# Cross-attention operands of a two-layer decoder: projected unpadded and placed by DMA, against projected in place with padding

## The reference, cut to what matters

```python
# x (2, 512, 256), ctx (2, 1024, 192); 16 heads in both attentions
x = layernorm(x + L0_attn(x))      # causal, 3-wide heads, geo bias
x = layernorm(x + L0_xattn(x, ctx))
def L0_xattn(query, kv):           # D = 16, scale = D ** -0.5
    q = (query @ Wq + bq).reshape(B, 512, 16, 16)
    k = (kv @ Wk + bk).reshape(B, 1024, 16, 16)
    v = (kv @ Wv + bv).reshape(B, 1024, 16, 16)
    attn = softmax(clip(q k^T * scale, -10000, 10000))
    return (attn v) @ Wo + bo
```

## Time and profile before

| | us |
|---|---|
| median of 3 runs (1264.87 to 1274.17) | 1266.02 |
| the profiled execution | 1272.5 |
| its span, first to last instruction | 1270.6 |
| PE busy | 1150.3 (91%) |
| DVE busy | 719.7 (57%) |
| ACT busy | 565.0 (44%) |
| POOL busy | 105.4 (8%) |
| cross-attention's last maximum (L1454) begins | 513.4 |

### The profile page before, as it was taken

The page is one execution under the profiler, slowest core; times in us unless marked ns, Lnnn a source line. Parts: engine busy times, 40 slices in busy tenths (PEclk is TensorE's granted clock), DMA queues, the critical chain, the costliest instruction groups (busy, mean ns, idle before and its releaser), DMA issues.

```text
span 1270.6 us, 19991 instructions
## 1 busy us (share of the span) xinstructions
PE 1150.3 (91%) x7418; PEld 720.2 (57%) x7418; DVE 719.7 (57%) x1054; ACT 565.0 (44%) x1084; POOL 105.4 (8%) x147
## 2 busy tenths in 40 slices
PE   4999999898988988869988999999999999998797
PEld 2453443442222322247866777877787887786465
DVE  4344445667888789661426466465646666673213
ACT  1344344154545555751214566456635564562210
POOL 0112232112100000010001000010001000100100
PEclk7799899898979999979999999999999999999799
DMA  7012212320000000000023233123634964400000
GB/s 205 14 51 100 89 37 100 115 76 1 1 1 1 1 1 1 1 18 1 1 67 112 62 91 74 34 52 83 150 85 100 214 144 101 101 18 1 1 17 17
DMA packets 56962, 74.20 MB, mean 58 GB/s; under 512 B 12443, under 2 KB 33446, under 8 KB 56870
## 3 DMA queue, kind: packets, MB, share of 16 engines
q1 hardware_dynamic: 53110, 69.26, 21.4%
q10 hardware_dynamic: 3760, 3.67, 0.9%
HBM read 36.20 MB, written 15.73 MB: 41 GB/s over the span
## 4 chain that ended last, share of the span: by engine, by line
PE 79%; DVE 9%; issue 5%; ACT 4%; DMA 1%; POOL 1%; SPq 1%; ACTq 0%; POOLq 0%; DVEq 0%
PE p_unit L1665 20%; PE p_ring L1665 12%; PE p_out L1789 9%; PE p_ring L1685 8%; PE p_ring L1766 8%; PE p_ring L1732 7%; PE p_out L1755 6%; DVE halves L1454 2%; PE p_unit L1857 2%; PE p_ring L1710 1%; ACT prob_b L1238 1%; DVE prob_a L1468 1%; DVE x L1560 1%; PE p_ring L1724 1%; PE p_ring L1703 1%
## 5 line engine op out<-in xcount | busy, mean ns | idle before, releaser
L1454 DVE TENSOR_REDUCE halves<-p_ring 128x2 f32<-128x1024 f32 x128 | 156.2, 1220 | 65.8 <-PE p_ring L1710 65.6
L1252 ACT ACTIVATE prob_a<-p_ring 128x1024 f32<-128x1024 f32 x128 | 130.6, 1022 | 101.6 <-PE p_ring L1732 101.4
L1434 DVE TENSOR_REDUCE nmax<-p_ring 128x2 f32<-128x1024 f32 (+1 forms) x128 | 156.0, 1219 | 33.7 <-PE p_ring L1685 33.6
L1270 ACT ACTIVATE probT_b<-p_ring 128x512 f32<-128x512 f32 x144 | 84.5, 598 | 202.2 <-PE p_ring L1766 200.7
L1238 ACT ACTIVATE prob_b<-p_ring,nmax 128x512 f32<-128x512 f32 (+1 forms) x192 | 158.6, 837 | 18.3 <-DVE nmax L1434 18.0
L1685 PE MATMUL p_ring<-stacks 128*128 128x512 f32 x512 | 151.4, 418 | 8.9 <-ACT prob_b L1238 5.3
L1487 DVE COPY probT_b<-p_ring 128x512 f32<-128x512 f32 x112 | 77.1, 688 | 133.5 <-PE p_ring L1766 133.0
L1766 PE MATMUL p_ring<-ident,prob_b 128*128 128x128 f32 x1024 | 134.5, 274 | 0.3 <-ACT probT_b L1270 0.3
L1766 PEld LDWEIGHTS p_ring<-ident,prob_b 128*128 128x128 f32 x1024 | 116.2, 141 | 23.5 <-issue 14.8
L1732 PE MATMUL p_ring<-x_q,x_kq 32*128 32x512 f32 x512 | 124.4, 658 | 2.9 <-DVE halves L1454 2.9
L1454 DVE TENSOR_REDUCE wide_max<-p_ring 128x2 f32<-128x256 f32 (+3 forms) x64 | 52.6, 823 | 90.3 <-PE p_ring L1703 90.3
(11 more groups left out here) (226 smaller groups left out, 1614.1 us busy)
## 6 DMA issues: line engine op xcount, KB each, us to landing
stacks<-x_kd SPq DMA_DIRECT2D x64, 256.0 KB, 5.9
stacks<-splitH_b SPq DMA_DIRECT2D x80, 128.0 KB, 2.3
stacks<-splitL_b SPq DMA_DIRECT2D x80, 128.0 KB, 2.4
x_kd<-early SPq DMA_DIRECT2D x19, 256.0 KB, 2.0
x_v<-x_vd SPq DMA_DIRECT2D x8, 512.0 KB, 4.1
x_kd<-xT SPq DMA_DIRECT2D x13, 256.0 KB, 2.0
x_vd<-early SPq DMA_DIRECT2D x11, 256.0 KB, 2.0
a_st<-a_image SPq DMA_DIRECT2D x64, 32.0 KB, 1.8
```

Of the source, the lines that this page charges most:

```text
L1252: nc.scalar.activation(prob_place(key), slot_of("S2", key), ACT.Exp, accum_out=x0_sums[:, m:m + 1]).then_inc(done["E2"], 1)
L1270: keep_turned(act, key, lambda o, i: nc.scalar.activation(o, i, ACT.Copy)).then_inc(done["VA"], 1)
L1434: nc.vector.tensor_reduce(nmax[:, n % 4, 0:heads], src, AX.X, ALU.max, negate=True).then_inc(done["M"], 1)
L1454: nc.vector.tensor_reduce(to, src, AX.X, ALU.max, negate=True).then_inc(done["M1"], 1)
```

## The change

Keys and queries are projected with the weights as they come, unpadded: a key unit "kd" yields 128 rows (8 heads) by 512 keys, a query unit "qd" 128 rows by 512 queries. That makes 4 key units and 2 query units per batch. The keys go through an early place to DRAM (x0_kd, step XO), the queries stay in x0_qd; the scale is applied when ACT empties them. A new step KL on SP places a group: for each head one DMA for 16 rows of 1024 keys and one for 16 rows of 512 queries. GpSimd clears x0_kq once, to 1 where keys go and 0 where queries go, and casts a whole group in one instruction of 1536 columns (KF). The four key units of batch 0 take the turns of the first four before; those of batch 1 stand at the head of x1_context. A query unit of batch 1 waits until the KL that read the same half of batch 0 is three turns old. The padded weights, their staging tiles, their clearing and most of XW go. The matmuls of A0's scores read 32 rows, not 17. X0's scores read 32 rows before and after; the rows of keys that were 0 are now 1, against 0 in the queries.

```diff
--- before.py
+++ after.py
@@ -168,7 +168,7 @@
-        return age("KF", "q", L, b, g) >= 2 and all(age("KF", "k", L, b, g, h) >= 2 for h in range(2))
+        return age("KF", b, g) >= 2
...
-            if u[0] in ("k", "q") and u[1] == "X0":
-                sched.add("KF", *u)
-            if u[:2] == ("v", "X1"):
+            if u[:2] == ("v", "X1") or u[0] == "kd":
                 sched.add("XO", *u)
...
-    def x0_keys(b, g):
+    def x0_keys(b):
+        return [unit("kd", b, m, s) for m in range(2) for s in range(2)]
+
+    def x0_queries(b):
+        return [unit("qd", b, m, after=[turned_x("A0", b)] + ([later(("KL", (0, 2 * m + 1)), 3)] if b else [])) for m in range(2)]
+
+    def x0_operands(b, g):
         n = 4 * b + g - HELD
-        return [unit("k", "X0", b, g, h, after=used(8 + n) if n >= 0 else []) for h in range(2)]
-
-    def x0_queries(b, g):
-        n = 4 * b + g - HELD
-        return [unit("q", "X0", b, g, after=[turned_x("A0", b)] + (used(8 + n) if n >= 0 else []))]
+        return [step("KL", b, g, after=[UA("qd", b, g // 2), later(("XO", ("kd", b, g // 2, 1)), 1)]
+                     + (used(8 + n) if n >= 0 else [])),
+                step("KF", b, g, after=[later(("KL", (b, g)), 2)])]
...
+        order = [u[1][1:] for u in x0_keys(1)] + order
...
-        [unit("cT", sg, c) for sg in range(2) for c in range(2)] + x0_keys(0, 0) + x0_keys(0, 1)
-        + [unit("cT", sg, c) for sg in range(2, 4) for c in range(2)] + x0_keys(0, 2)
-        + x0_keys(0, 3) + [u for g in range(4) for u in x0_keys(1, g)],
-        [q for b in range(B) for g in range(4) for q in x0_queries(b, g)],
+        [unit("cT", sg, c) for sg in range(2) for c in range(2)] + x0_keys(0)
+        + [unit("cT", sg, c) for sg in range(2, 4) for c in range(2)],
+        [q for b in range(B) for q in x0_queries(b)],
+        [s for b in range(B) for g in range(4) for s in x0_operands(b, g)],
...
-                slot = sum(early_uses) % EARLY
+                slot = sum(early_uses) % (3 if u[:2] == ("kd", 0) else EARLY)
...
-        x0_wq = put("x0_wq", [128, 2, 512])
-        x0_wk0 = put("x0_wk0", [128, 512])
-        x0_wk1 = put("x0_wk1", [128, 512])
+        x0_wq = put("x0_wq", [128, 2, C])
+        x0_wk0 = put("x0_wk0", [128, C])
+        x0_wk1 = put("x0_wk1", [128, C])
+        x0_qd = put("x0_qd", [128, 2, T])
...
+        x0_kd = nc.dram_tensor("x0_kd", (B, C, NKV), F32).ap()
...
-        X0_LOADS = 12
+        X0_LOADS = 9
...
-            sp.dma_start(wq_in[:, :, :], rows("L0_xattn_Wq")).then_inc(x0_loaded, 16)
-            sp.dma_start(wk_in[:, 0, :], d["L0_xattn_Wk"][0:128, :]).then_inc(x0_loaded, 16)
-            sp.dma_start(wk_in[0:CC - 128, 1, :], d["L0_xattn_Wk"][128:CC, :]).then_inc(x0_loaded, 16)
-            sp.dma_start(wk_in[64:65, 1, :], d["L0_xattn_bk"].rearrange("(o n) -> o n", o=1)).then_inc(x0_loaded, 16)
+            sp.dma_start(x0_wq[:, :, :], rows("L0_xattn_Wq")).then_inc(x0_loaded, 16)
             sp.wait_ge(pads_cleared, 1)
-            sp.dma_start(x0_wv0[:, 0:C], d["L0_xattn_Wv"][0:128, :]).then_inc(x0_loaded, 16)
-            sp.dma_start(x0_wv1[0:CC - 128, 0:C], d["L0_xattn_Wv"][128:CC, :]).then_inc(x0_loaded, 16)
-            sp.dma_start(x0_wv1[64:65, 0:C], d["L0_xattn_bv"].rearrange("(o n) -> o n", o=1)).then_inc(x0_loaded, 16)
-            bq = d["L0_xattn_bq"].rearrange("(g a p) -> a p g", a=4, p=16)
-            for a in range(4):
-                sp.dma_start(x0_bq[32 * a:32 * a + 16, :], bq[a], allow_slow_non_contiguous=True).then_inc(x0_loaded, 16)
+            for w0, w1, n in ((x0_wk0, x0_wk1, "k"), (x0_wv0, x0_wv1, "v")):
+                sp.dma_start(w0[:, 0:C], d["L0_xattn_W" + n][0:128, :]).then_inc(x0_loaded, 16)
+                sp.dma_start(w1[0:CC - 128, 0:C], d["L0_xattn_W" + n][128:CC, :]).then_inc(x0_loaded, 16)
+                sp.dma_start(w1[64:65, 0:C], d["L0_xattn_b" + n].rearrange("(o n) -> o n", o=1)).then_inc(x0_loaded, 16)
+            sp.dma_start(x0_bq[:, :], d["L0_xattn_bq"].rearrange("(m p) -> p m", p=128),
+                         allow_slow_non_contiguous=True).then_inc(x0_loaded, 16)
...
                 if kind == "XO":
+                    if u[0] == "kd":
+                        _, b, m, s = u
+                        wait(sp, "UA", *u)
+                        sp.dma_start(x0_kd[b, 128 * m:128 * m + 128, 512 * s:512 * s + 512], early_place(u, 0))\
+                          .then_inc(early_out[early_places[(u, 0)][0]], 16)
+                    elif u[0] == "v":
...
-                        for part, ready in ((1, "EH"), (0, "EL")):
-                            wait(sp, ready, *u)
+                        wait(sp, "EL", *u)
+                        for part in (1, 0):
                             sp.dma_start(x1_kd[b, p, 1 - part, :, 512 * s:512 * s + 512], early_place(u, part))\
                               .then_inc(early_out[early_places[(u, part)][0]], 16)
+                if kind == "KL":
+                    b, g = key
+                    G, place = 8 + 4 * b + g, (4 * b + g) % HELD
+                    sp.wait_ge(x0_cleared, 1)
+                    for s in range(2):
+                        slot, before = early_places[(("kd", b, g // 2, s), 0)]
+                        sp.wait_ge(early_out[slot], 16 * (before + 1))
+                    wait(sp, "UA", "qd", b, g // 2)
+                    if 4 * b + g >= HELD:
+                        wait(sp, "S2", *prob_items(PAIRS[G - HELD])[-1])
+                    for a in range(4):
+                        sp.dma_start(x0_kq[32 * a:32 * a + 16, place, 0:2, :],
+                                     x0_kd[b, 64 * g + 16 * a:64 * g + 16 * a + 16, :].rearrange("r (s n) -> r s n", s=2))\
+                          .then_inc(x0_held[place], 16)
+                        at = 64 * (g % 2) + 16 * a
+                        sp.dma_start(x0_kq[32 * a:32 * a + 16, place, 2, :], x0_qd[at:at + 16, g // 2, :])\
+                          .then_inc(x0_held[place], 16)
...
             blank(a0_v).then_inc(values_cleared, 1)
-            pool.wait_ge(x0_scaled, 1)
+            nc.gpsimd.memset(x0_kq[:, :, 0:2, :], 1.0)
+            nc.gpsimd.memset(x0_kq[:, :, 2, :], 0.0).then_inc(x0_cleared, 1)
             blank(x0_v).then_inc(values_cleared, 1)
...
                 if kind == "KF":
-                    u = key
-                    _, L, b, g = u[:4]
-                    place, part = (4 * b + g) % HELD, u[4] if u[0] == "k" else 2
-                    wait(pool, "UA", *u)
-                    if 4 * b + g >= HELD:
-                        wait(pool, "S1", *max_items(PAIRS[8 + 4 * b + g - HELD])[-1])
-                    nc.gpsimd.tensor_copy(x0_kqF[:, place, part, :], x0_kq[:, place, part, :]).then_inc(done["KF"], 1)
+                    b, g = key
+                    n = 4 * b + g
+                    pool.wait_ge(x0_held[n % HELD], 16 * 8 * (n // HELD + 1))
+                    if n >= HELD:
+                        wait(pool, "S1", *max_items(PAIRS[8 + n - HELD])[-1])
+                    nc.gpsimd.tensor_copy(x0_kqF[:, n % HELD], x0_kq[:, n % HELD]).then_inc(done["KF"], 1)
...
-                    elif u[0] in ("q", "k") and u[1] == "X0":
-                        _, L, b, g = u[:4]
-                        place, part = (4 * b + g) % HELD, u[4] if u[0] == "k" else 2
-                        if 4 * b + g >= HELD:
-                            wait(act, "S2", *prob_items(PAIRS[8 + 4 * b + g - HELD])[-1])
-                        if u[0] == "q":
-                            ins = nc.scalar.activation(x0_kq[:, place, part, :], p_unit[:, :], ACT.Identity,
-                                                       bias=x0_bq[:, g:g + 1])
-                        else:
-                            ins = nc.scalar.activation(x0_kq[:, place, part, :], p_unit[:, :], ACT.Copy)
-                    elif u[:2] in (("k", "X1"), ("v", "X1")):
+                    elif u[0] == "qd":
+                        _, b, m = u
+                        act.wait_ge(x0_scaled, 1)
+                        if b:
+                            for g in (2 * m, 2 * m + 1):
+                                act.wait_ge(x0_held[g % HELD], 16 * 8 * (g // HELD + 1))
+                        ins = nc.scalar.activation(x0_qd[:, m, :], p_unit[:, :], ACT.Identity, bias=x0_bq[:, m:m + 1],
+                                                   scale=LAYERS["X0"]["D"] ** -0.5)
+                    elif u[:2] in (("k", "X1"), ("v", "X1")) or u[0] == "kd":
                         early_free(act, u, 0)
                         ins = nc.scalar.activation(early_place(u, 0), p_unit[:, :], ACT.Copy)
...
-            for t in (x0_wv0, x0_wv1):
+            for t in (x0_wk1, x0_wv0):
                 nc.vector.memset(t[:, :], 0.0)
-            nc.vector.memset(x0_bq[:, :], 0.0).then_inc(pads_cleared, 1)
+            nc.vector.memset(x0_wv1[:, :], 0.0).then_inc(pads_cleared, 1)
...
-            nc.vector.memset(x0_wq[:, :, :], 0.0)
```

(37 more changed lines are left out.)

22 lines of the change are left out of this document (4 added, 18 removed).

## The result

| | us | ratio to the kernel before |
|---|---|---|
| before, median beside the changed kernel | 1266.9 | |
| changed, median of 4 runs (1235.13 to 1245.31) | 1239.1 | 0.977 [0.975, 0.980] |
| changed, second comparison (a1_after) | 1243.2 | 0.980 [0.977, 0.983] |
| changed, third comparison (a2_after) | 1240.2 | 0.978 [0.975, 0.981] |

The change gains 24 to 28 us. I forecast 14.7, with a range that reached to a gain of 24 (1242 us).

What follows compares the result with a forecast made beforehand. PE was taken to bound self-attention, DVE cross-attention from about 300 us. Terms -22.1 + 1.4 + 3.4 - 1.8 + 4.4 gave -14.7 us, a predicted median of 1251.3 us; 8-in-10 range 1242 to 1263.

Steps and rivals of the forecast that it cites:

- -22.1 + 1.4 + 4.4: DVE-bound cross-attention: products gone -22.1 us, one query product of batch 1 coming back at turn 107 +1.4, casts +4.4.
- What bounds the kernel: PE bounds self-attention (60 to 200 us), DVE cross-attention from about 300; windows: DVE busy 29.79 of 31, 29.62 of 35 us.
- Products gone from five blocks: Cross-attention, turns 104 to 168: all 15 key and query products leave, saving 22.1 us (bounds 20.9 and 23.9).
- Early products: PE-bound part: seven products added, five removed, net 3.4 us more (bounds 0 and 7.6).
- Start: DVE's weight clears no longer precede the subtraction before the first scatter: 1.8 us gained (bounds 0.7 and 2.2).
- The cast: Cross-attention: GpSimd's merged 1.84 us cast locks out DVE's clip, 1.1 us each, four counted: +4.4 us (bounds 0 and 9.2).
- 32 rows: Self-attention score matmuls: 32 rows take 0.50 us against 0.49 for 17, so nothing (bounds 0 and 2.6 us).
- Rival C: Better than forecast: casts fall into DVE's holes, early products hide, or PE keeps full clock; 1242 us; chance 0.17.
- Rival A: Two or three of the five cross-attention casts stop PE and its clock falls: 1260 to 1264 us; chance 0.17.
- B: At turns 64 to 68 group loads hold SP and ACT waits for early slots: up to 10 us, 1261; chance 0.06.
- D: All five casts take their full 1.84 us and bring a half-clock spell: 1277.6 us, slower than before; chance 0.04.
- E: Cross-attention products were hidden and something else sets the 4.26 us per block, so no gain: 1273 us; chance 0.02.

Runs made afterwards that it cites:

- e2: The changed kernel with the self-attention's score matmuls over 17 rows again instead of 32; ratio to the kernel before 0.9813.
- e10: e6 with the self-attention's score matmuls over 17 rows instead of 32; 1237.0 us, 0.976 of the kernel before.
- e12: e9 with the self-attention's score matmuls over 17 rows instead of 32; 1237.6 us, 9.0 us slower than a3 beside it.
- e3: The kernel before with DVE's clears of the padded weights moved ahead of its wait for the first weights; 1265.14 us, 0.9982.
- e11: The kernel before with the self-attention's score matmuls over 8 rows instead of 17; 1267.5 us, 1.000.
- e1: The kernel before with the self-attention's score matmuls over 32 rows instead of 17; 1264.14 against 1267.66 us, 0.9968.
- e5: The changed kernel with each whole-group GpSimd cast made twice, one after the other; 1241.5 us, 0.980 of the kernel before.
- e6: The changed kernel with KS, the GpSimd instruction scaling a later layer's weights, cut into four pieces; 1234.4 us, 0.9738 of the kernel before.
- e7: The changed kernel with KS, the GpSimd scaling of a later layer's weights, put behind the last exponential in step order; 1238.5 us, 0.9775.
- e4: The changed kernel without the four key products of batch 1 (part of the output left wrong); 1240.6 us, 0.978 of the kernel before.
- e8: The changed kernel with each of the four key products of batch 1 made twice on PE; 1245.6 us, 0.983 of the kernel before.
- e13: The changed kernel with the self-attention's score matmuls over 8 rows instead of 32; 10.9 us slower than the changed kernel beside it.
- e9: e6 with GpSimd's 128x1024 additions cut into pieces as well; 1231.0 us, 0.970 of the kernel before.
- a3: e9 run again, unchanged, beside its twin with 17 rows; 1228.6 us, 0.968 of the kernel before.

## Why the forecast missed

Two terms of the sum failed: the casts' +4.4 us, which cost nothing, and the wider rows' 0, which gained. The same two stretches, as means over the traces, against the sum's terms:

```
                                    forecast   measured
start                                  -1.8      -1.4   first maximum 31.5 -> 29.8 to 30.4
turns 6-102, without the wider rows    +3.4      +3.3   256.0 (3 traces) -> 259.3 (e2, e10, e12)
turns 6-102, 17 -> 32 rows                0      -5.9   259.3 -> 253.4 (6 traces)
turns 102-197                         -16.3     -20.2   220.4 (4 traces) -> 200.2 (8 traces)
sum                                   -14.7     -24.2
```

Of the kernel before, the 3 traces are its own, e3 and e11, the 4 those and e1. With the change, the 6 are its own three, e5, e6 and e7; the 8 are its own three, e2, e4, e5, e8 and e13. The stretch 102 to 197 of the forecast is -22.1 + 1.4 + 4.4. The sum is close to what the three medians show (-24.4 to -28.0). The terms are less sure than it: single traces of one kernel differ by up to 5.7 us in a stretch (254.0 to 259.7 before), and with e13 (8 rows, 266.8), which the table leaves out, the second and third rows would read +5.2 and -7.8.

- **What bounds the kernel**: right. The two limits, and the pair of windows that separates them, carried the whole prediction.
- **Products gone from five blocks**: right. For the third to fifth I had 4.26 us each; the 15 turns around them went from 33.22 to 28.79, 36.42 to 32.17 and 33.22 to 28.78, that is 4.43, 4.25 and 4.44.
- **Early products, +3.4**: near in size, in part by luck. Of the 3.3 us, turns 96 to 102 hold 1.9 (18.4 us before, 20.7 in e2 and e10, 19.5 in e12), and 1.3 to 1.9 of the 2.3 there go when GpSimd's additions are cut (e9, a3): the shifted work makes a DVE instruction meet them, a lock that the sum didn't have. What is left for the products is smaller than forecast, and no run prices it.
- **Start, -1.8**: right, with e3 alone 1.9 us in the trace.
- **The cast, +4.4: wrong, it is 0.** Three steps of it failed, the last of them the one that decides. The duration: three times 0.61 us overstates one instruction three times as wide (1.46 us), since each of the three carries a fixed part. The start: I let a cast begin at random in the turn and took a mean delay of 1.1 us; it mostly began early in a maximum, and the mean was 0.58 (0 to 1.27). And the payment: I added each delay to the end, though the same window showed DVE idle 1.2 us of 31. A delay no longer than the slack up to the next block is given back, as the clip 1.27 us late shows, and e5 with 0.5 to 1.4 us at each pair of casts. The lock itself was right: the clips of 1 to 3 us that I had named as its sign came (1.04 to 1.95 us, but for one), and the cost did not. That a merged cast is worse than three short ones, as I had concluded from it, did not show in the time: even two merged ones cost nothing.
- **32 rows, 0: wrong, and in the traces the largest miss** (5.9 us; 4 us in e1's time and 0.3 to 9 in the pairs with the change, so its size is open). I costed it by the length of one matmul (0.49 and 0.50 us), and that bound could not contain a gain at all. Rival C named the mechanism ("the wider rows ... keep PE at full clock") and gave it no number in the range beyond 1242, only 1.8 us for each product mended. A bound from rows was at hand: before, 10.3 us between 100 and 200 us were at half clock (148.6 to 155.4, 192.9 to 196.4), and a PE-bound stretch loses up to half of that, 5.1 us; the measured 5.9 has stretches outside of this part in it too.
- **Rival A** (casts pull the clock down) fell for four of the five casts: no stretch at half clock follows them but the one behind KS, which is gone in e6 with the cast still there. Behind the first, 4 of the 14 traces with the change (a1_after, e2, e8, e13) have one of 3.4 us, 13 to 14 us later, which lengthens turns 108 to 118 from 20.6 to 21.9 us; a DVE instruction of 2.28 us stands between, and no run separates the two. e7 shows what brought a stretch by itself: 4.7 us of lock. **B** (SP's queue) did not occur: ACT waits for no DMA between 60 and 230 us in the traces of the changed kernel and a1_after. Nor did **D** and **E**. **C** was the case that came, in both its forms: casts in the holes, and the rows.

The gain of the fastest version comes from the same lock: KS and the additions in pieces, 1228.6 to 1231.0 us, 0.968 [0.965, 0.971] and 0.970 [0.968, 0.973], some 9 to 12 us below the changed kernel. The rule of the Trainium skill (SBUF — State Buffer, "SBUF: two separate sides") that the pair of ports is locked for the whole instruction pays here, and not at the cast. The trace agrees: the same work in four pieces let a clip in between each two.

## What to carry to other kernels

Before adding up delays, look up the slack of the engine that is delayed: a stall below it costs nothing (0.58 us on average here, up to 1.27), one well above it costs itself (4.8 us for a clip of 4.7 us) and can bring a stretch at half clock on top. So cut GpSimd instructions that run beside a DVE-bound loop into pieces that each delay it by less than that slack (here 1.8 us each; clips beside them were 0.12 to 0.17 us late). And an edit that changes no duration is not bounded by zero while PE is the limit and the trace shows stretches at half clock there: half of their length is a first estimate of what it may move.

## What the runs showed of the hardware

- The rows that the score matmuls read went with the granted clock, not with their length: 32 rows for 17 gave 0.9968 [0.9954, 0.9982] in the kernel before, and in the fastest version 1228.6 for 1237.6 us at a mean clock of 0.982 for 0.973; but 0.3 us between e2 and a1_after, and 8 for 17 gave 1.000 in the kernel before. Why is open.
- GpSimd's cast to fp32r takes 0.61 us for 512 columns and 1.46 for 1536: 0.18 us fixed and 0.83 ns a column, an estimate from these two.
- Between two GpSimd instructions that followed one another DVE got its clip in: the second cast then took 1.81 instead of 1.46 us, and the four pieces of 512 columns 7.18 us, where the one of 2048 took 5.69 (part of this is the pieces' own fixed time). DVE's turns kept their length (28.79 us for 15 with one cast and with two).
- A place in an order of steps holds back only engines that wait there: GpSimd ran e7's moved step at 427.4 us, 52 us before the last maximum, though it was put behind the last exponential.
